# A macaron block's attention with every engine's order laid out anew, TensorE's code without a loop, and the squares of q and k on GpSimd

## The reference

```python
x = x + 0.5 * ffn(_layernorm(x), w_gate, w_up, w_down)
x = x + attn(_layernorm(x), norm_w, Wq, Wk, Wv, Wo, gate, log_temperature)
x = x + 0.5 * ffn(_layernorm(x), w_gate, w_up, w_down)

def attn(x, ...):                       # 4 heads of 32 for q, 2 for k and v
    h = x * rsqrt(mean(x * x) + 1e-6) * norm_w
    q, k, v = h @ Wq, h @ Wk, h @ Wv    # split in heads, k and v repeated
    q = q / max(norm(q), 1e-12)         # per row and head
    k = k / max(norm(k), 1e-12)
    p = softmax(causal(q @ k.T * exp(log_temperature)))
    return x + gate * ((p @ v) @ Wo)

def ffn(x, ...):                        # hidden 384, weights int32 / 127
    return (silu(x @ wg.T) * (x @ wu.T)) @ wd.T
```

## Time and profile before

| | |
|---|---|
| median of three runs | 443.08 us (442.51 to 443.92) |
| the profiled execution | 444.12 us |
| its span | 442.3 us |
| first feed-forward and weights | to 103.6 us of the span |
| attention, first to last exponential | 103.6 to 359.05 us |
| busy: TensorE, ScalarE, VectorE, GpSimd | 91, 84, 80, 58% |
| exponentials on ScalarE | 144 of 1125 ns, 154.0 us |

### The profile page before, as it was taken

One profiled execution on the slowest core, in us unless ns is written; L12 is line 12 of the kernel. 1 busy time (PEld: TensorE's weight loads), 2 busy tenths in 40 slices (PEclk: granted clock), 3 DMA queues, 4 the chain that ended last, 5 costly groups with the idle time before them and its releaser, 6 DMA issues.

```text
span 442.3 us, 12788 instructions
## 1 busy us (share of the span) xinstructions
PE 400.9 (91%) x4899; PEld 215.4 (49%) x4899; DVE 355.6 (80%) x943; ACT 371.2 (84%) x497; POOL 255.9 (58%) x325
## 2 busy tenths in 40 slices
PE   0689998989896999996999999999999999999994
PEld 0346565664442534533535535435445345676654
DVE  5989997799799796996696996996967958888654
ACT  3899999776896798895799899898988999999950
POOL 5789999984626414634334624633132558999850
PEclk9999999999999899998899999999999999999999
DMA  6586443416236028037009127046052115465442
GB/s 166 128 172 154 50 61 61 95 23 109 64 66 118 11 51 138 9 73 124 1 10 149 37 40 153 4 73 122 1 95 52 25 25 87 105 127 115 110 105 76
DMA packets 119230, 35.21 MB, mean 80 GB/s; under 512 B 101632, under 2 KB 119168, under 8 KB 119168
## 3 DMA queue, kind: packets, MB, share of 16 engines
q1 hardware_dynamic: 117888, 34.02, 40.3%
q10 hardware_dynamic: 1280, 0.33, 0.3%
HBM read 4.98 MB, written 4.19 MB: 21 GB/s over the span
## 4 chain that ended last, share of the span: by engine, by line
PE 54%; DVE 12%; ACT 11%; issue 7%; POOL 7%; DMA 7%; SPq 1%; ACTq 0%; DVEq 0%
PE ps L724 11%; PE ps L507 10%; PE ps L754 9%; PE ps L761 9%; ACT PT L867 4%; PE ps L787 4%; PE ps L571 4%; PE ps L560 3%; DMA AXT<-AS 3%; ACT XN L459 3%; DVE H L328 2%; PE ps L731 2%; PE ps L596 2%; POOL HL L434 2%; DVE RD L241 1%
## 5 line engine op out<-in xcount | busy, mean ns | idle before, releaser
L867 ACT ACTIVATE PT<-ps,k_exp 128x1024 f32<-128x1024 f32 x144 | 154.0, 1125 | 13.7 <-PE ps L731 11.2
L507 PE MATMUL ps<-XT,WT 128*128 128x512 f16 x384 | 94.1, 384 | 6.0 <-DMA XT<-w_int 2.1
L724 PE MATMUL ps<-QKT 128*32 128x512 f16 (+1 forms) x1280 | 90.3, 364 | 9.3 <-issue 4.4
L754 PE MATMUL ps<-PT,V 128*32 128x512 f32 (+3 forms) x768 | 77.6, 495 | 0.0
L761 PE MATMUL ps<-PT,ones 128*32 128x512 f32 (+3 forms) x768 | 76.0, 486 | 0.0
L434 POOL TENSOR_TENSOR HL<-H,HH 128x1024 f16<-128x1024 f32 x31 | 66.5, 2146 | 8.1 <-ACT HH L483 5.3
L328 DVE SCALAR_TENSOR_TENSOR H<-SG,k_isilu,ps 128x1536 f32<-128x1536 f32 x32 | 57.9, 1808 | 13.9 <-ACT SG L477 5.7
L999 POOL TENSOR_TENSOR ST<-QN,ST 128x512 f16<-128x512 f32 x16 | 19.3, 1208 | 71.5 <-ACT ST L899 71.5
L507 PEld LDWEIGHTS ps<-XT,WT 128*128 128x128 f16 x384 | 34.5, 98 | 50.6 <-issue 11.5
L724 PEld LDWEIGHTS ps<-QKT 128*32 128x32 f16 x1280 | 29.5, 96 | 56.2 <-ACT PT L867 26.9
L459 ACT ACTIVATE XN<-X,NB,RS 128x128 f32<-128x128 f32 x128 | 52.4, 483 | 3.1 <-POOL NB L406 3.0
(11 more groups left out here) (139 smaller groups left out, 660.2 us busy)
## 6 DMA issues: line engine op xcount, KB each, us to landing
result<-X SPq DMA_DIRECT2D x15, 256.0 KB, 2.5
X<-in_L_attn_x SPq DMA_DIRECT2D x7, 512.0 KB, 4.3
X<-in_L_attn_x SPq DMA_DIRECT2D x2, 256.0 KB, 4.7
XT<-w_int SPq DMA_TRANSPOSE x32, 3.1
QKT<-ST SPq DMA_TRANSPOSE x18, 5.9
AXT<-AS SPq DMA_TRANSPOSE x16, 2.9
w_int<-in_L_ffn_w_gate SPq DMA_DIRECT2D x1, 192.0 KB, 4.2
w_int<-in_L_ffn_w_up SPq DMA_DIRECT2D x1, 192.0 KB, 4.4
```

The lines of the kernel that those rows point to most:

```text
L507: i = e.matmul(out[:, j, :], WT[:, wp, w * NJ + j, :], XT[k % 2][:, xp, :], start=a == 0, stop=a == len(passes) - 1)
L724: i_ = e.matmul(dst[r, :].rearrange("p (s a n) -> p s a n", a=2, n=P), QKT[k % 2][:, i // TPC, NH + hp, key0 + r.start:key0 + r.stop], q.r ...
L754: e.matmul(sums_of(h, 0, n), V[k % 2][:, i, v0:v0 + HD], weights_of(g, h, o, n), start=i == 0, stop=i >= TPC * qc, skip_group_check=True)
L867: e.activation(dst, SCORES[(SLOT0[g] + i) % 2][:, :, :], ACT.Exp, scale=k_exp[:, 0:1]).then_inc(a_exp, 1)
```

## The change

The work is the same; where it stands in each engine's list is not. GpSimd makes the squares by a product of q and k with themselves (`tensor_tensor`) in place of ScalarE's activation. For the first batch's squares, which are made in the first feed-forward stage, ScalarE keeps them. TensorE's steps are written out for all eight batches. The last projection, ("qkv", 1, 1), stands behind group 2 and not 1, ("wo", 1) behind group 3 and not 2. On VectorE the stats of a chunk are taken one step earlier, at a step's end, and the division of the last sums comes first in a step. SyncE issues half 1 of `QKT` behind both `AXT` transposes from the second batch on.

```diff
-        USES = {0: [("qkv", 0, 0), ("qkv", 0, 1)], 1: [("qkv", 1, 0), ("qkv", 1, 1)],
-                2: [("wo", 1)], 7: [("rows", 0)], 9: [("wo", 0), ("rows", 1)]}
+        USES = {0: [("qkv", 0, 0), ("qkv", 0, 1)], 1: [("qkv", 1, 0)], 2: [("qkv", 1, 1)],
+                3: [("wo", 1)], 7: [("rows", 0)], 9: [("wo", 0), ("rows", 1)]}
...
-            drive(e, step, B, 1, 3)
+            if shift:
+                drive(e, step, B, 1, 3)
+            else:
+                for k in range(B):
+                    step(k, k)
...
# ScalarE, att_act
-                    if g == 8:
+                    if g == 6:
                         o_hi(e, b * 2)
...
-                        g_ = g - 2 if k == 0 else g
-                        if g_ == 0:
-                            qkv_out(k + 1, m0, k, b, 0)
-                        elif g_ == 1:
+                        if g == (2 if k == 0 else 0):
                             for c in range(2):
+                                v_out(k + 1, m0, k, b, 0, c)
+                        for c, at in enumerate((3, 3) if k == 0 else (1, 2)):
+                            if g == at:
                                 v_out(k + 1, m0 + 1, k, b, 1, c)
-                        if g == (4 if k == 0 else G0):
-                            squares(k + 1, m0 + 1, k, b, 1)
-                        for half, at in enumerate((4, 6) if k else (5, 7)):
-                            if g == at:
-                                stack_hi(m0 + half, half)
-                    if k + 2 < B and g == NG - 2:
+                        if g == 4:
+                            stack_hi(m0, 0)
+                        if g == 8:
+                            stack_hi(m0 + 1, 1)
+                    if k + 2 < B and g == 7:
                         x_hi(m0 + 2, 0)
                         x_hi(m0 + 3, 1)
...
# GpSimd, att_pool
+            def squares(kk, m, k, b, half):
+
+                await_read(e, k, b, ("qkv", half, 1))
+                e.wait_ge(a_ss, 2 * m - 1)
+                qk = V[kk % 2][:, half * TPC:half * TPC + TPC, 0:DQ + DK]
+                e.tensor_tensor(SQ[:, :, :], qk, qk, ALU.mult).then_inc(a_sq, 1)
...
# VectorE, att_dve
-                if later:
+                if k == 0:
                     stats(m0 + 2, m0 + 2, q)
+                    stats(m0 + 3, m0 + 3, q + 1)
                 if k >= 1:
                     o_norm(e, b * 2 - 1)
                 if not nxt:
                     ffn_dve(e, 1, [("moments", c) for c in range(4)])
-                if later:
-                    stats(m0 + 3, m0 + 3, q + 1)
+                if later and k >= 1:
+                    normalise(m0 + 2, m0 + 2, q)
                 if nxt:
                     sums(m0, 0)
                     norms(20 * b + 20, 4 * b + 6, 0, 1)
                     unit(k + 1, 20 * b + 30, m0, 0)
+                o_norm(e, b * 2, k == 0)
+                if k == 0:
+                    stack_hi2(m0, 0)
+                    normalise(m0 + 2, m0 + 2, q)
+                if later:
+                    normalise(m0 + 3, m0 + 3, q + 1)
                 if k >= 1:
                     wo_out(k, b, ("wo", 1), b * 2 - 1)
-                o_norm(e, b * 2, k == 0)
+                if nxt and k >= 1:
+                    stack_hi2(m0, 0)
                 if nxt:
                     sums(m0 + 1, 1)
-                    stack_hi2(m0, 0)
                     norms(20 * b + 30, 4 * b + 8, 1, 2)
                     unit(k + 1, 20 * b + 40, m0 + 1, 1)
                 if later:
-                    normalise(m0 + 2, m0 + 2, q)
-                    normalise(m0 + 3, m0 + 3, q + 1)
-                if nxt:
-                    stack_hi2(m0 + 1, 1)
+                    add_norm(m0 + 2, m0 + 2, q)
+                    add_norm(m0 + 3, m0 + 3, q + 1)
                 if nxt:
                     rows(m0, k, b, 0)
+                    stack_hi2(m0 + 1, 1)
+                if k + 3 < B:
+                    stats(m0 + 4, m0 + 4, 2 - q)
+                    stats(m0 + 5, m0 + 5, 3 - q)
...
```

More of the change, by code:

```diff
@@ L612, in macaron_kernel @@
         G0 = len(row_groups(0))
-        USES = {0: [("qkv", 0, 0), ("qkv", 0, 1)], 1: [("qkv", 1, 0), ("qkv", 1, 1)],
-                2: [("wo", 1)], 7: [("rows", 0)], 9: [("wo", 0), ("rows", 1)]}
-        MOVED = {0: [], 1: [], 2: USES[0], 3: USES[1]}
+        USES = {0: [("qkv", 0, 0), ("qkv", 0, 1)], 1: [("qkv", 1, 0)], 2: [("qkv", 1, 1)],
+                3: [("wo", 1)], 7: [("rows", 0)], 9: [("wo", 0), ("rows", 1)]}
+        MOVED = {0: [], 1: [], 2: USES[0], 3: USES[1] + USES[2]}
         FIRST = [("qkv", h, c) for h in range(2) for c in range(2)] + [("rows", 0)]
@@ L874, in x_hi @@
                 e.activation(AS[half][:, 0, :, :], AN[half][:, :, :], ACT.Copy).then_inc(a_xh, 1)
-            def qkv_out(kk, m, k, b, half):
-                for c in range(2):
-                    v_out(kk, m, k, b, half, c)
-                squares(kk, m, k, b, half)
             def v_out(kk, m, k, b, half, c):
@@ L961, in att_pool @@
         def att_pool(e, first=None):
+            await_read = bank_uses(False)[2]
+            def squares(kk, m, k, b, half):
[3 more added lines that the diff above has]
+                e.tensor_tensor(SQ[:, :, :], qk, qk, ALU.mult).then_inc(a_sq, 1)
             def rstds(m, q):
@@ L1018, in step @@
                     rstds(m0 + 2, q)
+                    rstds(m0 + 3, q + 1)
+                if nxt:
+                    squares(k + 1, m0, k, b, 0)
                 if k >= 1:
                     o_lo(e, b * 2 - 1)
+                if nxt:
+                    squares(k + 1, m0 + 1, k, b, 1)
                 if not nxt:
@@ L1023, in step @@
                                     ("x_hi", 1), ("x_lo", 1)])
-                if later:
-                    rstds(m0 + 3, q + 1)
                 if nxt:
                     stack_lo(m0, 0)
-                    stack_lo(m0 + 1, 1)
                 o_lo(e, b * 2)
@@ L1032, in step @@
                     x_lo(m0 + 3, 1)
+                if nxt:
+                    stack_lo(m0 + 1, 1)
                 if not nxt:
@@ L1245, in step @@
                     wo_out(k, b, ("wo", 0), b * 2)
-                if later:
-                    add_norm(m0 + 2, m0 + 2, q)
-                    add_norm(m0 + 3, m0 + 3, q + 1)
-                if nxt:
                     rows(m0 + 1, k, b, 1)
@@ L1307, in turn @@
             for k in range(B):
-                for half in range(2):
-                    qk(2 * k + half)
+                qk(2 * k)
+                if k == 0:
+                    qk(1)
                 for half in range(2):
@@ L1312, in turn @@
                         turn_x(e, 2 * k + 2 + half)
+                if k:
+                    qk(2 * k + 1)
         on_all = [[0, P], [1, 1]]
```

## The result

The changed kernel takes 450.44 us, the median of four runs (450.10 to 450.85), where the kernel before takes 443.08. The ratio is 1.0165, with an interval of 1.0146 to 1.0184. The forecast of 433.1 us and its range, 429.5 to 439.5, are both missed, on the wrong side of no change. The profiled execution took 450.58 us, its span 448.8.

What follows compares the result with a forecast made beforehand. TensorE was taken as the bound. Won 6.7 us (batch 3), 2.8 (batches 2, 4, 5, 6), 3.9 (batch 1); lost 3.0 (batch 0), 0.4 (batch 7): 10.0 off 443.08, so 433.1 us, range 429.5 to 439.5.

Steps and rivals of the forecast that it cites:

- TensorE's loop goes: Attention, between batches 2 and 3: without the loop's branch, the pause and slow clock behind it vanish, worth 5.6 us.
- A steady batch: Batches 2, 4, 5, 6: less waiting of TensorE as ScalarE is relieved, 30.3 us each, 2.8 us won together.
- rival 3: GpSimd's squares block VectorE, giving it 29.5 us of work in a 30.3 us batch: 439 us, chance 0.08.
- The sign that the prediction named for being wrong: Steady batches: the forecast is wrong if ScalarE waits there for V or QN; no size given.
- The cover for QN: Each batch: QN is ready at 14 us, ScalarE's copy of it stands at about 18, so 4 us of cover.
- Transposes: AXT ahead of QKT's second half: batch 1's 2.33 us wait goes, QKT stays hidden, batch 7 loses 0.4 us.
- Batch 0: First attention batch: squares behind GpSimd's second rstds, ScalarE idles 4 us for QN, 3.0 us lost.
- Chances: Odds given to the outcomes: faster 0.90, no change 0.03, slower 0.07; the forecast itself 0.58.

Runs made afterwards that it cites:

- e1: The kernel before, with TensorE's eight attention batches written out and nothing else: 439.33 us, ratio 0.9882.
- e2: The changed kernel with ScalarE making the 14 squares again, all else as changed: 434.89 us, ratio 0.9789.
- e11: The changed kernel with GpSimd squaring 32 of 768 elements, every wait and instruction kept: 437.90 us, ratio 0.9842.
- e12: e2 plus, on GpSimd in the squares' places, a product of 768 elements that nobody waits for: 447.92 us, ratio 1.0064.
- e9: e2 with add_norm one step later, ScalarE's last ST copy two groups earlier and VectorE's attention steps written out: 436.77 us, ratio 0.985.
- e10: e2 with VectorE's attention steps written out too: 433.34 us, ratio 0.9764.
- e6: The changed kernel with GpSimd's first squares of batch 0 between the two rstds, not behind both: 447.99 us, ratio 1.0078.

## Why the prediction was wrong

**TensorE's loop goes.** Right in kind. No uncaused wait stands between batches 2 and 3, and e1 puts the edit alone at 4.5 us (forecast 5.6). In the changed kernel nothing of it is left to see, since batch 3 came to 32.4 us, not 30.3, for another reason.

**A steady batch.** This step failed. It asked what holds TensorE and answered ScalarE; it freed ScalarE of 2.8 us, laid 3.3 more on GpSimd, and left VectorE's time as it was. Batches 1 to 5 took 32.4 to 33.6 us, because VectorE, held beside GpSimd's instructions, is busy for 31.2 to 32.3 us of each. Over the whole span the squares cost 15.5 us (e2), of which some 12.5 go with the time in which they are in work (e11), and 13.0 come with a product that nobody waits for (e12). The mechanism is that of rival 3, which had a chance of 0.08 and 439 us. The sign that the prediction named for being wrong is there: ScalarE waits for QN in steady batches, as at 305.23 (9.5 us in batches 1 to 6; 0.6 in e2).

**Why rival 3 was priced too low.** It charged VectorE 3.3 us a batch for the squares. Measured by batch 5 it is 2.3 (29.7 to 32.0), so this part was high. But it began from today's 26.2 us, and in the new order VectorE stands at 29.7 before any squares (e2), because add_norm and others meet GpSimd's low parts. 29.5 of 30.3 seemed just to fit; 32.0 does not. The row that would have told was there: normalising at 3.42 and 5.15 us for the same eight instructions, which by the pair at 296.70 take about 2.1 alone (0.34, and 0.25 for each further one). I read it as a risk to the squares only, and not as a price for every instruction of VectorE that the new order puts beside GpSimd. Held here are instructions that read two tensors in SBUF (R<-RT,R, up to 1.09 us for 0.18), but also some that read one (normalising, add_norm, the limit, R<-SS). I had counted on the first alone and taken most of VectorE's list to be safe. QN, the one that rival 3 named, takes 958 ns in the mean in the changed kernel and was not held there (in e9 it was: 1344). The Trainium skill, "SBUF — State Buffer", section on its two separate sides, names two kinds of VectorE instruction that exclude a GpSimd one: with two SBUF inputs, or in a two-port mode. The prediction took over only the first, and by that half the trace doesn't agree. No row here shows an instruction's mode, so whether the held ones with one tensor are of the second kind is open.

**The cover for QN.** I had QN at 14 us into a batch, 4 us ahead of its copy, with the rstds right behind the low part at 1.6 us in. They waited for VectorE's stats and began at 277.44, 4.3 us in, another wait for VectorE that I had put at nothing. So in batch 5 GpSimd's second rstds end at 283.6, 10.5 us in and not 7.8, and the first QN ends at 18.9, a us before its copy: the cover was used up there, and the second QN was 1.9 us late.

**Transposes.** AXT's wait went, right. QKT's second half was in time for the fourth group from batch 1 on. The waits that came are for the first half, at a batch's start: five, 6.0 of the 7.7 us. I had looked at the issue of the second only. The last batch took 28.4 us and not 27.4, in e2 and e10 too. TensorE's first 8 us there match (the 16 matmuls start at 7.5 us in), so the transpose is not the cause. The trace of that batch has two places where ScalarE's exponentials fall behind those of before: 0.5 us for `o_hi`, which now stands ahead of the last ones, and a wait of 0.95 us at 351.15 for scores that TensorE issues behind the output product of batch 6, which has moved there. No run tests either.

**Batch 0.** ScalarE idled 5.2 us for the first QN (forecast 4) and TensorE behind it 4.5, which starts again at half clock (granted 0.50 from 129.4 to 131 us):

```profile
127.53 0.84 ACT L898 ACTIVATE ST<-QN 128x768 f16<-128x768 f32 x1 [5.17 <-DVE QN L1147]
```

```profile
129.43 1.04 PE L724 MATMUL ps<-QKT 128*32 128x512 f16 x8 [4.52 <-ACT PT L871]
```

The batch took 3.9 us more, forecast 3.0; e6 confirms that GpSimd's order is the cause.

**How near e2 comes.** With the squares back on ScalarE the rest of the change takes 434.9. That is close to 433.1, but partly by errors that cancel: batch 0 takes 31.3 us there, with no loss at all, while batch 1 takes 32.4 against 30.3, and steady batches 30.8 against 30.3.

**Chances.** 0.90 for faster rested on TensorE's and ScalarE's rows. The sum had no term for VectorE, the engine with the most work moved beside GpSimd's.

## What to carry to other kernels

Here 14 squares of 1.47 us, 20.6 in all, added 10.5 us to VectorE in the new order and 3.4 in the old one. What counts is whether VectorE has that much to spare in a batch, and the sum has to be done for the new neighbours of an order as well as for new instructions. A product that nobody waits for, in the places of the planned work, prices that before the work is moved. And a loop's branch is looked for on every engine again after each change of order, since its pause came and went here with the order around it.

## What the hardware showed beyond this

Instructions of VectorE that read one SBUF tensor were held beside GpSimd's, down to 24 elements a partition. Around the second squares of batch 0, and the same instruction a little later with GpSimd idle:

```profile
123.05 1.47 POOL L967 TENSOR_TENSOR SQ<-V 128x768 f32<-128x768 f32 x1 [1.13 <-DVE SS L1093]
128.45 1.16 POOL L1006 TENSOR_TENSOR ST<-QN,ST 128x512 f16<-128x512 f32 x1 [3.94 <-ACT ST L898]
```

```profile
123.21 1.33 DVE L1102 TENSOR_SCALAR R<-SS 128x24 int32<-128x24 int32 x1
...
127.41 3.34 DVE L241 RECIPROCAL RD<-PVS 128x512 f32<-128x512 f32 x1
...
135.96 0.18 DVE L1102 TENSOR_SCALAR R<-SS 128x24 int32<-128x24 int32 x1
```

R<-SS ends with the squares. The reciprocal beside GpSimd's low part of the stack takes the 3.34 us that it always takes. The pause at a branch took 4.39 us on TensorE in one kernel and 2.07 in another, and 6.86 on VectorE in one and nothing that shows in e2: the loop and its count of passes are the same, what differs is the order inside it. What in the order sets the pause, no run shows.
